# Layer 0 attention: value products of two groups in one PSUM tile, the early mask inside VectorE's maximum, late scores directly behind their mask

## The reference

```python
h = layernorm(x)
qvk = (h @ Wqvk).reshape(b, s, 3, 16, 8)             # q, v, k; 16 heads of depth 8
scores = einsum('bshi,bthi->bsth', q, k) + causal_mask   # -inf above the diagonal
weights = softmax(scores / sqrt(128), axis=2)
wv = einsum('bsth,bthi->bshi', weights, v).reshape(b, s, 128)
x = x + wv @ Wo + experts_top2(h)                    # layer 0
x = x + retention(layernorm(x)) + gated_experts(layernorm(x))   # layer 1
```

## Time and profile before

| | us |
|---|---|
| median of 3 runs | 783.85 |
| the runs | 783.3, 783.85, 787.15 |
| span of the profiled execution, first to last instruction | 765.3 |
| TensorE busy in it | 703.9 (92%) |
| VectorE busy | 546.6 (71%) |
| ScalarE busy | 419.5 (55%) |
| GpSimd busy | 327.7 (43%) |

### The profile page before, as it was taken

The page is one execution under the profiler, slowest core; times in us unless marked ns, Lnnn a source line. Parts: engine busy times, 40 slices in busy tenths (PEclk is TensorE's granted clock), DMA queues, the critical chain, the costliest instruction groups (busy, mean ns, idle before and its releaser), DMA issues.

```text
span 765.3 us, 17690 instructions
## 1 busy us (share of the span) xinstructions
PE 703.9 (92%) x6133; PEld 526.3 (69%) x6133; DVE 546.6 (71%) x1053; ACT 419.5 (55%) x802; POOL 327.7 (43%) x433
## 2 busy tenths in 40 slices
PE   5787788998899978989898999999999999999997
PEld 4643445556755547757666888888888888888885
DVE  6878997885678866779886766666665666666665
ACT  5645665676477678677664444444444444444442
POOL 3765643783758860147694631212122221222222
PEclk9999999999999999999999999999999999999999
DMA  6984655431134420012114611112121212111100
GB/s 188 261 239 137 179 133 201 167 95 49 51 120 129 142 85 1 12 33 61 54 43 117 156 52 56 56 41 69 41 69 41 69 41 59 50 52 58 41 15 14
DMA packets 63795, 66.51 MB, mean 87 GB/s; under 512 B 6512, under 2 KB 41840, under 8 KB 63728
## 3 DMA queue, kind: packets, MB, share of 16 engines
q1 hardware_dynamic: 62128, 63.23, 27.7%
q0 software_dynamic: 1024, 2.12, 1.0%
q10 hardware_dynamic: 576, 0.27, 0.1%
HBM read 47.46 MB, written 17.99 MB: 86 GB/s over the span
## 4 chain that ended last, share of the span: by engine, by line
PE 75%; DVE 9%; issue 5%; ACT 4%; DMA 3%; POOL 2%; SPq 1%; ACTq 0%; POOLq 0%; DVEq 0%
PE ps L1763 25%; PE ps L1992 22%; PE ps L1876 3%; DVE m L1241 3%; PE ps L1683 3%; PE ps L1587 3%; PE ps L1796 2%; PE ps L1831 2%; PE ps L1593 2%; PE ps L1597 2%; PE ps L1897 1%; DMA qk_parts<-qk_p 1%; PE ps L1601 1%; PE ps L1688 1%; PE ps L1580 1%
## 5 line engine op out<-in xcount | busy, mean ns | idle before, releaser
L963 ACT ACTIVATE f_h<-ps 128x512 fp32r<-128x512 f32 x256 | 153.3, 599 | 197.6 <-PE ps L1763 197.6
L1463 DVE SCALAR_TENSOR_TENSOR f_l<-ps,f_h 128x512 fp32r<-128x512 f32 x256 | 175.9, 691 | 112.5 <-ACT f_h L963 111.3
L1763 PE MATMUL ps<-x_hl,w_h 128*128 (+1 forms) x512 | 200.3, 391 | 0.0
L783 POOL TENSOR_TENSOR acc<-acc,yt 128x512 f32<-128x512 f32 x55 | 70.9, 1289 | 249.8 <-DVE yt L1501 249.8
L877 ACT ACTIVATE probs<-ps 128x1536 f32<-128x1536 f32 x64 | 92.8, 1450 | 34.4 <-PE ps L1606 33.8
L1763 PEld LDWEIGHTS ps<-x_hl,w_h 128*128 128x128 f32 x512 | 96.1, 188 | 19.6
L682 POOL TENSOR_SCALAR_AFFINE_SELECT probs<-probs 128x512 f32<-128x512 f32 x128 | 78.4, 637 | 59.8 <-ACT probs L877 59.5
L1992 PE MATMUL ps<-f_l,w_h 128*128 128x512 f32 x256 | 99.8, 390 | 1.3 <-DVE f_l L1463 1.3
L1992 PE MATMUL ps<-f_h,w_h 128*128 128x512 f32 x256 | 99.7, 390 | 0.0
L1763 PE MATMUL ps<-x_hl,w_l 128*128 (+1 forms) x256 | 99.6, 389 | 0.0
L1992 PE MATMUL ps<-f_h,w_l 128*128 128x512 f32 x256 | 99.6, 389 | 0.0
(11 more groups left out here) (225 smaller groups left out, 1328.2 us busy)
## 6 DMA issues: line engine op xcount, KB each, us to landing
gate_b<-gate_rows SPq DMA_DIRECT2D x64, 256.0 KB, 3.3
qk_parts<-qk_p SPq DMA_DIRECT2D x16, 512.0 KB, 3.8
k_st<-qk_parts SPq DMA_DIRECT2D x64, 96.0 KB
q_st<-qk_parts SPq DMA_DIRECT2D x64, 96.0 KB
y_tok<-zero SPq DMA_DIRECT2D x8, 512.0 KB, 2.9
w_raw<-in_w_e SPq DMA_DIRECT2D x16, 256.0 KB, 2.7
x_rows<-xn_rows SPq DMA_DIRECT2D x8, 260.0 KB, 3.2
w_up<-in_w_up SPq DMA_DIRECT2D x8, 256.0 KB, 2.7
```

The costliest lines, as they stand in the source:

```text
L783: nc.gpsimd.tensor_tensor(acc[:, :], acc[:, :], yt[:, e % 2, :], ALU.add).then_inc(summed, 1)
L963: nc.scalar.activation(r32(f_h[:, m % 4, :]), ps[:, m % 4, :], ACT.Relu).then_inc(f_hi, 1)
L1463: nc.vector.scalar_tensor_tensor(out=r32(f_l[:, m % 4, :]), in0=ps[:, m % 4, :], scalar=0.0, in1=f_h[:, m % 4, :], op0=ALU.max, op1=ALU.su ...
L1763: last = nc.tensor.matmul(dst, r32(lhs[i]), r32(rhs[j]), start=(k == 0), stop=(k == 2))
```

## The change

Values: v_ring gets 48 columns for a pair of heads: eight values and a one, zeros, eight values and a one at column 32. A group takes 32 of them, the first or the last, so that even groups fill rows 0 to 15 and odd groups rows 16 to 31 of each head's 32-row tile, and both accumulate in one tile. Evacuation, transpose and division are done once for two groups. The early mask on TensorE is dropped; VectorE adds the mask and takes the maximum in one instruction for each head. Late scores follow their mask; the transposed maxima go to bank 0; the order in scores() is new. Two head transposes are done in one slot. The order of heads in the query and key weights (by_depth) follows.

```diff
-        def heads_turned(b, t):
-            return 4 * b + 8 + (t if b < B - 2 else 0)
+        def heads_turned(b):
+            return 4 * b + 8
-        ps_m = ps[0:2 * GH, 6, S:S + P]
+        ps_m = ps[0:2 * GH, 0, 0:P]
...
-            def evacuate(g):
-                act.wait_ge(pv_done, num(g) + 1)
-                if past(g, 2):
-                    act.wait_ge(o_turned, num(g) - 1)
-                nc.scalar.activation(o_ring[:, at(g, 2), :], ps_o, ACT.Copy).then_inc(o_evac, 1)
+            def evacuate_pair(i):
+                act.wait_ge(pv_done, 2 * i + 2)
+                if i >= 2:
+                    act.wait_ge(o_turned, i - 1)
+                nc.scalar.activation(o_ring[:, i % 2, :], ps_o, ACT.Copy).then_inc(o_evac, 1)
...
-                if past(g, 3) and within(plus(g, -3), G0):
-                    evacuate(plus(g, -3))
+                if num(g) % 2 == 0 and 4 <= num(g) <= G0 + 2:
+                    evacuate_pair(num(g) // 2 - 2)
...
                 dve.wait_ge(early_done, num(g) + 1)
                 first = 3 if ahead_of_all(g) else 0
-                nc.vector.tensor_reduce(m8[:, at(g, 2), :, 0], ps[:, first, :].rearrange("p (h k) -> p h k", h=GH), AX.X, ALU.max).then_inc(early_max, 1)
+                if past(g, 1):
+                    dve.wait_ge(early_max, num(g))
+                else:
+                    dve.wait_ge(consts_ready, 5)
+                for h in range(GH):
+                    last = nc.vector.tensor_tensor_reduce(out=masked_qk[:, h, :], in0=ps[:, first, h * P:(h + 1) * P], in1=later_keys[:, :], scale=1.0,
+                                                          scalar=float(NEG), op0=ALU.add, op1=ALU.max, accum_out=m8[:, at(g, 2), h, 0:1])
+                last.then_inc(early_max, 1)
...
-                if n >= 4 and within(plus(g, -4), G0):
-                    divide(plus(g, -4))
+                if n % 2 == 1 and 5 <= n <= G0 + 3:
+                    divide_pair((n - 5) // 2)
...
-            def mask_early(g):
+            def early_free(g):
                 if past(g, 2):
-                    pe.wait_ge(early_max, before_it(g))
-                nc.tensor.matmul(scores_at(g)(0).rearrange("p (h k) -> p h k", h=GH), ident_h[:, :],
-                                 mask_qk[:, :].unsqueeze(1).broadcast_to([P, GH, P]), start=True, stop=False, skip_group_check=True)
+                    pe.wait_ge(mneg_done, num(g))
...
+            def late_scores(far):
+                if at(far, RING) % 2 == 0:
+                    pe.wait_ge(stack_in[at(far, RING) // 2], div(far, RING) * 64 + 64)
+                for n in range(2):
+                    for u in range(2):
+                        last = late(far, u, n)
+                last.then_inc(late_done, 1)
...
             def scores(g):
                 far = plus(g, 3)
                 both = within(far, G0)
-                if both:
-                    if at(far, RING) % 2 == 0:
-                        pe.wait_ge(stack_in[at(far, RING) // 2], div(far, RING) * 64 + 64)
-                    for n in range(2):
-                        for u in range(2):
-                            last = late(far, u, n)
-                    last.then_inc(late_done, 1)
                 if past(g, 1):
                     pe.wait_ge(exp_done, num(g))
...
                 pe.wait_ge(mrow_in[at(g, 4)], div(g, 4) * 16 + 16)
+                for u in range(2):
+                    turned_first(g, u, 0)
+                if both:
+                    early_free(far)
                 for n in range(2):
                     if both:
                         left = early(far, 0, n)
                     right = turned_second(g, 1, n)
...
-                for n in range(2):
-                    for u in range(2):
-                        turned_first(g, u, n)
+                for u in range(2):
+                    turned_first(g, u, 1)
...
             def weigh(g):
-                if past(g, 1):
-                    pe.wait_ge(o_evac, num(g))
-                pe.wait_ge(mneg_done, min(n + 3, G0))
-                if n >= 8 and n % GPB0 < TB:
-                    pe.wait_ge(wvn_done, (n - 8) // GPB0 * TB + (n % GPB0 + 1 if n < G0 else TB))
+                if num(g) % 2 == 0 and num(g) >= 2:
+                    pe.wait_ge(o_evac, num(g) // 2)
+                if n >= 8 and n % GPB0 == 0:
+                    pe.wait_ge(wvn_done, (n - 8) // GPB0 * TB + TB)
+                rows = slice(k % 2 * 2 * HD0, k % 2 * 2 * HD0 + 4 * HD0)
                 for h in range(GH):
-                    nc.tensor.matmul(ps_o[32 * h:32 * h + 2 * HD0, :], v_ring[:, u, 0, k * GH + h, :],
+                    nc.tensor.matmul(ps_o[32 * h:32 * h + 4 * HD0, :], v_ring[:, u, 0, k // 2 * GH + h, rows],
                                      probs[:, at(g, HELD), 1 + h // 2, h % 2 * S:(h % 2 + 1) * S],
-                                     start=True, stop=False, skip_group_check=True)
+                                     start=(k % 2 == 0), stop=False, skip_group_check=True)
...
             for n in range(3):
+                if n == 2:
+                    turn_max((0, 1))
+                    keep_on(7, 2)
                 scores_alone((0, n))
-                if n:
+                if n == 1:
                     keep_on(7, 2)
-                    turn_max((0, n - 1))
+                    turn_max((0, 0))
                     keep_on(7, 2)
...
             def slot(g):
+                if n == FIND:
+                    pe.wait_ge(wv_put, (FIND - 5) // 2)
+                    find_slots()
+                if n % 2 == 1 and 5 <= n <= G0 + 3:
+                    turn_out((n - 5) // 2)
                 if within(plus(g, 3), G0):
                     mask_late(plus(g, 3))
...
-                if n == FIND:
-                    pe.wait_ge(wv_put, FIND - 4)
-                    find_slots()
-                if past(g, 4) and within(plus(g, -4), G0):
-                    turn_out(plus(g, -4))
+                if within(plus(g, 3), G0):
+                    late_scores(plus(g, 3))
                 if within(plus(g, 2), G0):
                     turn_max(plus(g, 2))
-                if within(plus(g, 3), G0):
-                    mask_early(plus(g, 3))
                 if within(g, G0):
                     scores(g)
```

More of the change, by code:

```diff
@@ L163, in build @@
         qk_rest = sb("qk_rest", [P, 2, 2, S], where=era)
+        later_keys = sb("later_keys", [P, P], where=era)
+        masked_qk = sb("masked_qk", [P, GH, P], BF16, where=era)
         with ExitStack() as part:
@@ L884, in slot @@
                     act.wait_ge(rstd_ready, B + 2)
+                    act.wait_ge(pv_done, G0 - 1)
                     normalise(0, 0)
@@ L1592, in early @@
                 h = 2 * u + n
-                return nc.tensor.matmul(scores_at(g)(0)[:, h * P:(h + 1) * P], qs[:, 0:P], ks[:, 0:P], start=False, stop=True, skip_group_check=True)
+                return nc.tensor.matmul(scores_at(g)(0)[:, h * P:(h + 1) * P], qs[:, 0:P], ks[:, 0:P], start=True, stop=True, skip_group_check=True)
             def late(g, u, n):
@@ L1612, in scores_alone @@
                 mask_late(g)
-                mask_early(g)
+                early_free(g)
                 for n in range(2):
@@ L1787, in find_slots, with turn_out, turn_heads @@
                 last.then_inc(slots_mm, 1)
-            def turn_out(g):
-                pe.wait_ge(o_evac, num(g) + 1)
-                if past(g, 1):
-                    pe.wait_ge(wv_put, num(g))
-                if g[1] % GPB0 == 3 and past(g, 7):
-                    pe.wait_ge(x_attn, div(plus(g, -7), GPB0) + 1)
+            def turn_out(i):
+                pe.wait_ge(o_evac, i + 1)
+                if i >= 1:
+                    pe.wait_ge(wv_put, i)
+                if i % 2 == 1 and i >= 3:
+                    pe.wait_ge(x_attn, (i - 3) // 2 + 1)
                 for t in range(TB):
-                    last = nc.tensor.transpose(ps_tok[:, t * P:(t + 1) * P], o_ring[:, at(g, 2), t * P:(t + 1) * P], ident[:, :])
+                    last = nc.tensor.transpose(ps_tok[:, t * P:(t + 1) * P], o_ring[:, i % 2, t * P:(t + 1) * P], ident[:, :])
                 last.then_inc(o_turned, 1)
-            def turn_heads(b, t):
-                pe.wait_ge(wv_put, b * GPB0 + GPB0)
-                if heads_turned(b, t) >= G0 - 2:
-                    pe.wait_ge(o_evac, min(heads_turned(b, t) - 2, G0))
-                nc.tensor.transpose(ps_heads(t if b >= B - 2 else 0), wv_tok[:, b % 2, t, :], ident[:, :]).then_inc(wv_mm, 1)
+            def turn_heads(b):
+                pe.wait_ge(wv_put, (b + 1) * GPB0 // 2)
+                if heads_turned(b) >= G0 - 2:
+                    pe.wait_ge(o_evac, min(heads_turned(b) // 2 - 1, G0 // 2))
+                for t in range(TB):
+                    nc.tensor.transpose(ps_heads(t), wv_tok[:, b % 2, t, :], ident[:, :]).then_inc(wv_mm, 1)
             def attention_out(b):
                 pe.wait_ge(wvn_done, TB * (b + 1))
```

(2 more changed lines are left out.)

59 lines of the change are left out of this document (30 added, 29 removed).

## The result

The changed kernel takes 793.73 us (median of 4 runs, 792.36 to 796.08) beside 785.1 (783.3 to 787.15) for the kernel before in the same series: a ratio of 1.0114 [1.0096, 1.0133], slower by 1.1%. A second comparison gave 1.0141 [1.0108, 1.0175]. The forecast was 792 us with a range of 779 to 805.

A forecast was written before the change was run, and what follows sets the result against it. A cycle of waits was taken to bound layer 0's attention, TensorE's queue close behind. Quiet +5.5, routing -0.7, start +2.5, middle +0.7 gave +8.0 us on a 765.3 span, plus 18.55 outside: 792 us, range 779 to 805.

The forecast's parts named there:

- Steps 3 and 4: Layer 0's quiet slots: early scores wait for ScalarE's negation behind TensorE's queue; periods 3.03 against 2.88 us, +5.5 us.
- Step 5: VectorE's early maximum: four fused instructions at 0.28 us each, 1.12 to the next instruction, hidden behind TensorE's queue in quiet slots.
- rival with the cheap maximum: Fused maximum at 0.20 us each, routing slots fall to TensorE's floor: sum +3.4, 787 us; chance 0.20.
- Step 6: Routing slots, bound by VectorE: division in pairs and earlier output transposes against the dearer maximum, -0.7 us over 15 slots.
- Step 7: ScalarE's evacuation and head copies just fit behind the negation; value products with 32 output rows cost nothing: zero.
- Step 8: Start of layer 0's attention: dearer first maxima and group 2's scores behind the negation, +2.5 us; also the middle, +0.7.
- middle: The short period after the expert stage, 2.31 us, rises to the new period length: +0.7 us.
- would break the sum: Sign of error: a lower granted TensorE clock between 80 and 250 us, since TensorE idles more; no size given.
- time beside the span: The median of the runs lies 18.55 us above the profiled span of 765.3, and nothing changes there.
- dear maximum: Rival: fused maximum at 0.37 us each, release after 1.57; sum +19.6, 803 us; chance 0.16.
- covered hop: Rival: transposes of the maxima start before e+1.38, e the exponential's start; quiet slots 2.70, sum -9, 775 us; chance 0.16.
- first part: Late scores directly behind their mask cut VectorE's 2.77 us cycle, leaving TensorE's queue as bound: 2.68 less the early mask.

The follow-up runs named there:

- experiment 2: The kernel before with only the turned maxima moved to bank 0, so the early mask waits for ScalarE's negation: 795.56 us, ratio 1.0338.
- experiment 3: The changed kernel without the wait for the negation: maxima turned into bank 6, turned heads in bank 7, part of the result lost; 773.63 us, ratio 1.0047.
- second run: The changed kernel, unchanged, measured and profiled again beside the kernel before: 794.17 us, ratio 1.0141.
- experiment 8: The changed kernel with the value products' second half moved behind the transpose of the maxima in three slots of four: 790.36 us, ratio 1.0062.
- middle kernel of the table: The kernel before with only the late scores moved ahead of the transpose of the maxima, from the same series as the changed kernel's second run: ratio 0.9979.
- Experiment 9: The changed kernel with idle-time multiplications added while TensorE waits in the first slots of layer 0's attention: 792.26 us, ratio 1.0093.
- experiment 7: The kernel before with only the late scores moved directly behind their mask, ahead of the transpose of the maxima: 782.80 us, ratio 0.9979.
- Experiment 10: The changed kernel with no mask on TensorE or in the maxima and one plain early maximum: 801.0, 823.9, 799.3 and 840.2 us in four runs.
- experiment 1: The kernel before, unchanged, measured and profiled again: 770.62 us, ratio 1.0005.

## Why the prediction was right, and where it was not

The time was met (792 forecast, 793.7 measured), and the mechanism that it put on the path was the right one. But that the total fits is partly luck: the sum of +8.0 us holds errors of opposite sign. By its steps:

- **Steps 3 and 4, the hop over ScalarE and TensorE's queue: right.** Shown by the slot above (each offset within 0.03), by experiment 2 (0.53 a slot when added alone) and by experiment 3 (0.23 a slot when taken out). The quiet periods came to 3.05 instead of 3.03, since the mask follows the output transposes 0.04 later than taken. Exponential 42 to 61 took 58.0 us beside 55.4 before: 0.14 in each of 19 periods, 4.6 us over 34; forecast +5.5, where the prediction's own periods (3.03 against 2.88) give 5.1. The price of leaving the tiles, of which no row of before spoke, was 0.32 as taken.
- **Step 5, the fused maximum: mis-sized.** It was taken at 0.28 an instruction and measured 0.21 to 0.22: the lower bound (0.20), which only the rival with the cheap maximum used. The argument from neighbouring reductions that overlap by 0.09 was the one to trust; adding 0.08 for the second row was wrong, since that row lies beside the next instruction.
- **Step 6, routing slots: mis-sized by that term.** Forecast -0.7 us; measured 54.2 against 57.8, -3.6. With 0.21 in place of 0.28 the prediction's own working gives -0.16 - 0.4 + 0.25, -4.7 us over 15 slots, and the rival with the cheap maximum came closer with -4.6.
- **Step 7, nothing on ScalarE and in the value products: right.** 32 output rows instead of 16 are not seen: from the second value products to the mask it is 0.33, and was 0.35, and ScalarE's copies end within the slot.
- **Step 8, start: right in size by luck.** +2.5 us in the second run and +3.5 in the first, forecast +2.5. But the second run has 6.8 us at half clock there, and the same program without them in experiment 8 is at +1.2: the start was taken 1.3 us too long, and the clock, which has no term in it, filled the gap. The **middle** (+0.7) can't be told: 39 to 42 takes 43.9 beside 43.8 in the middle kernel of the table, and half-clock stretches that come and go there are larger than the term.
- **The missing term: TensorE's clock.** Exponentials 1 to 8 took 30.0 us instead of 23.3 to 23.8, +6.3 us. The prediction named a lower clock as what "would break the sum" and put nothing into the sum for it. Experiment 9 shows that 4.7 of the 6.3 us go when one wait of TensorE is filled, and in experiment 8 5.3 went with a shorter stretch. The remaining 1.6 us are not split up; the hop acts in these slots too, and the sum has no term for it there. The Trainium skill (TensorE: Matmul & The Clock Gate, "HAM oscillation — how this bites in real kernels") warns of waits for transfers that send the clock down again and again, and advises a loop in which TensorE is not left waiting. The traces agree in kind, with the fall at the end of the wait of 1.58 us, here one for VectorE; filling it removed one stretch while others came later.
- **The time beside the span: wrong, no harm.** The 18.55 us were not an overhead of each execution, but only 1.8 to 2.4 us of them.

Together: 4.6 (quiet) - 3.6 (routing) + 2.5 (start) + 6.3 (the first seven periods) is 9.8 us; the two ratios are worth 8.9 and 11.1 us. Of the 9.8 about 6.0 came with half clock (1.3 at the start, 4.7 in the first periods). Without them the change would have cost some 4 us, an estimate from these rows, near the +3.4 of the rival with the cheap maximum (787). So the forecast was right in its main term and in its total, and it owes the total to terms that were too high by 2.9 (routing), 1.3 (start), 0.9 (quiet) and 0.7 us (middle) against a missing 6.0 of half clock and 1.6 beside it. The terms are read from profiles of different series, so each is good to some tenths of a us only.

Of the rivals: the dear maximum is refuted by 0.21 an instruction. The covered hop is refuted by the transpose at e+1.53, where it needed e+1.38. What the change was to bring by its first part is worth 0.2% alone (experiment 7).

What stays open: why TensorE's clock comes back within 4 us in the kernel before, after a wait of 2.57 us (or does not fall at all), after 6.8 us in experiment 8, after a wait of 1.70, and only after 24 us in the changed kernel, after 1.58. At half clock TensorE is busy nearly all the time in each. Experiment 10 stays down for 68 us, so the answer is not simply how much work it has.

## What to carry to other kernels

Giving a small PSUM tile a bank that another product needs turns a copy on ScalarE into a link of TensorE's own cycle; here the way is 0.31 + 0.27 + 0.06 us long where 0.11 stood before, 0.53 us a slot and 3.4% of the time if nothing else is moved. Price the freed instruction against that before sharing the bank. Where a change lets TensorE wait somewhere new, put a term for its clock into the sum: a slot at half clock takes 4.15 us or more where one at full clock takes 3.0, and a wait of 1.58 us was followed by 24 us of such slots, one of 1.70 at the same place by 6.8. A term that was met may owe it to the clock, as the start did here: look at the granted clock of the stretch before calling it right.

## What the hardware showed that was not expected

- A custom VectorE operation on 128 columns from PSUM with a written maximum runs every 0.21 to 0.22 us at 0.285 us busy; the second row of 0.08 us lies beside the next instruction and adds nothing to that.
- The same program took 770.6 us in one series of runs and 785 in others, and the record has the same chip number for one of each. In the series at 785 us VectorE and ScalarE have waits of up to 4.4 us that the trace marks as remote, from exponential 39 to 42 in all eight profiles and from 24 to 39 in seven of them. The five other profiles have none, and 24 to 39 takes 42.8 us in experiment 1 beside 48.8 in experiment 7. That these waits are the whole of the 6 us is not shown: experiment 8 has none there and takes 48.8 too.
- With TensorE at half clock a slot of experiment 10 lasts 4.24 us, at full clock 2.80: it can stay in either for tens of us, and less work for TensorE was no protection.
